# Each product ahead of a row maximum is multiplied twice in the first batch of an attention block

## What is computed

```python
xn = layernorm(x)                              # over channels
q, k, v = split(xn @ Wqkv.T + bqkv)            # 16 heads of 16
q, k = rope(q), rope(k)
att = softmax(where(causal, q @ k.T / 4, -inf))
s = (att @ v) @ Wo.T + bo
g = silu(sum_r(xn @ factors[r]) / sqrt(8) + bias)
out = x + s * g
```

## Time and profile before

| | before |
|---|---|
| three runs, us | 259.08, 259.93, 257.48 |
| median, us | 259.08 |
| the profiled execution, its time, us | 259.9 |
| its span, us | 258.1 |
| busy: PE, DVE, ACT, POOL, us | 233.8, 187.8, 140.2, 105.2 |
| mean granted clock of TensorE | 0.94 |

### The profile page before, as it was taken

The page is one execution under the profiler, slowest core; times in us unless marked ns, Lnnn a source line. Parts: engine busy times, 40 slices in busy tenths (PEclk is TensorE's granted clock), DMA queues, the critical chain, the costliest instruction groups (busy, mean ns, idle before and its releaser), DMA issues.

```text
span 258.1 us, 4983 instructions
## 1 busy us (share of the span) xinstructions
PE 233.8 (91%) x1717; PEld 141.2 (55%) x1717; DVE 187.8 (73%) x622; ACT 140.2 (54%) x268; POOL 105.2 (41%) x85
## 2 busy tenths in 40 slices
PE   5599969899966799999999999999998999999982
PEld 2388845465633335646675557464854474474552
DVE  7579789914799959479997868799968696941124
ACT  2511814667530157468547596667266467748840
POOL 8107868950386030030087200943565016019900
PEclk9799999869995569999999999999999799999999
DMA  6996301551024033000003520151016200002002
GB/s 195 353 325 180 69 0 60 201 200 35 0 98 149 6 122 124 5 3 0 3 5 106 198 70 5 65 187 39 3 35 205 93 6 0 4 5 84 3 0 81
DMA packets 15788, 21.42 MB, mean 83 GB/s; under 512 B 2068, under 2 KB 9236, under 8 KB 15764
## 3 DMA queue, kind: packets, MB, share of 16 engines
q1 hardware_dynamic: 14704, 19.54, 23.0%
q10 hardware_dynamic: 868, 1.05, 1.4%
q0 software_dynamic: 192, 0.52, 0.9%
HBM read 6.16 MB, written 2.10 MB: 32 GB/s over the span
## 4 chain that ended last, share of the span: by engine, by line
PE 67%; DVE 22%; DMA 3%; issue 3%; ACT 3%; ACTq 0%; DVEq 0%
PE o_ps L460 14%; DVE ring_ps L756 13%; PE ring_ps L564 11%; PE ring_ps L519 8%; PE ring_ps L575 7%; PE ring_ps L534 7%; PE ring_ps L500 7%; PE ring_ps L470 3%; PE ring_ps L510 3%; DMA probs<-wqk 2%; DVE rowmax L760 2%; PE ring_ps L550 2%; DVE rowmax L756 2%; PE ring_ps L608 2%; PE ring_ps L493 2%
## 5 line engine op out<-in xcount | busy, mean ns | idle before, releaser
L756 DVE CUSTOM_DVE_ANT_0 ring_ps<-ring_ps,later_k 128x512 f32<-128x512 f32 (+3 forms) x224 | 106.8, 543 | 17.7 <-PE ring_ps L534 17.4
L870 ACT ACTIVATE probs<-ring_ps 128x512 f32<-128x512 f32 x160 | 84.5, 603 | 28.2 <-PE ring_ps L575 23.5
L534 PE MATMUL ring_ps<-stack_k,stack_q 62*128 62x512 f32 (+3 forms) x256 | 44.0, 400 | 5.8 <-DVE rowmax L756 3.9
L564 PE MATMUL ring_ps<-stack_q,stack_k 64*128 64x128 f32 (+3 forms) x256 | 40.5, 371 | 3.5 <-DVE rowmax L756 1.5
L460 PE MATMUL o_ps<-probs,vaug 128*17 128x256 f32 (+3 forms) x496 | 37.9, 447 | 0.0
L534 PEld LDWEIGHTS ring_ps<-stack_k,stack_q 62*128 62x128 f32 x256 | 22.8, 197 | 24.2 <-issue 8.3
L756 DVE DVE_READ_ACCUMULATOR2_ANT rowmax<- 128x1 f32 x224 | 31.7, 141 | 0.0
L641 POOL TENSOR_TENSOR parts<-parts,by_sin 128x512 f32<-128x512 f32 x7 | 9.1, 1303 | 54.4 <-DVE by_sin L737 54.4
L564 PEld LDWEIGHTS ring_ps<-stack_q,stack_k 64*128 64x128 f32 x256 | 22.4, 194 | 16.2 <-issue 8.2
L575 PE MATMUL ring_ps<-ident_bf,later_k 128*128 128x256 bf16 (+1 forms) x160 | 29.1, 265 | 0.0
L519 PE MATMUL ring_ps<-wvg_sb,xnT 128*128 128x512 f32 x96 | 26.3, 419 | 0.8 <-DVE by_sin L737 0.7
(11 more groups left out here) (89 smaller groups left out, 279.9 us busy)
## 6 DMA issues: line engine op xcount, KB each, us to landing
stack_q<-parts SPq DMA_DIRECT2D x48, 128.0 KB, 2.6
stack_k<-parts SPq DMA_DIRECT2D x42, 128.0 KB, 2.6
probs<-factors SPq DMA_DIRECT2D x2, 1024.0 KB, 10.0
out<-result SPq DMA_DIRECT2D x8, 256.0 KB, 2.3
xbuf<-x SPq DMA_DIRECT2D x3, 512.0 KB, 8.2
xbuf<-x SPq DMA_DIRECT2D x2, 256.0 KB, 2.9
probs<-wqk ACTq DMA_DIRECT2D x2, 256.0 KB, 6.4
stack_k<-parts POOLq DMA_DIRECT2D x4, 128.0 KB, 3.8
```

The source lines that it names most:

```text
L534: mm = pe.matmul(ps[:, s * width:(s + 1) * width], qk[b % 2][0][rows, h // SIDES, tile * P:(tile + 1) * P], qk[b % 2][1][rows, h // SIDES, ...
L564: pe.matmul(ps[:, col:col + T - j * P], qk[b % 2][1][side(h), h // SIDES, j * P:(j + 1) * P], qk[b % 2][0][side(h), h // SIDES, j * P:T], ...
L756: last = dve.tensor_tensor_reduce(scores, scores, later_k[:, T - width:], 1.0, LOWEST, ALU.add, ALU.max, rowmax[:, tile, unit, column + s: ...
L870: act.activation(probs[:, chunk % PROB_SLOTS, :], ps[:, :], ACT.Exp, scale=float(HD) ** -0.5).then_inc(taken[kind], 1)
```

## The change

A table `REPEAT` gives, for each batch, how often the products of a maxima step are multiplied. In batch 0 it is 2, in the others 1. The extra products have the same operands and go to the same place in the same bank, just ahead of the old ones. As the old ones begin with `start=True`, they overwrite what the extra ones left, which nobody reads. No semaphore is added or moved.

```diff
--- before.py
+++ after.py
@@ -58,6 +58,7 @@
 
 WARM_UP = 12
 KEEP_WARM = 5
+REPEAT = (2, 1, 1, 1)
 VECTOR_MASKS_FROM = 1
 MAX_CHUNKS = 12
 EXP_CHUNKS = 10
@@ -526,6 +527,13 @@
                     wait_bank(pe, (kind, b, i + 1))
                     both = [(ring_bank((kind, b, n)), *max_chunk(n // MAX_CHUNKS, n % MAX_CHUNKS)) for n in (i, i + 1)]
                     count_heads = len(both[0][2])
+                    for s in [s for _ in range(REPEAT[b] - 1) for s in range(count_heads)]:
+                        for ps, tile, heads in both:
+                            h, width = heads[s], (tile + 1) * P
+                            rows = slice(side(h).start, side(h).start + DOT_ROWS)
+                            pe.matmul(ps[:, s * width:(s + 1) * width],
+                                      qk[b % 2][0][rows, h // SIDES, tile * P:(tile + 1) * P],
+                                      qk[b % 2][1][rows, h // SIDES, 0:width], start=(s == 0), stop=(s == count_heads - 1))
                     for s in range(count_heads):
                         for ps, tile, heads in both:
                             h, width = heads[s], (tile + 1) * P
```

## The result

The changed kernel takes 262.71 us, the median of four runs (261.75 to 263.43), beside 258.88 for the kernel before, also four runs (257.48 to 259.93). The ratio is 1.0164, with a 95% interval of 1.0118 to 1.0209: slower by 3.8 us, where the forecast was 258.3 us, 0.8 less than the 259.08 known then, and outside the range. A second series on another chip gave 1.0141 (1.0070 to 1.0212). The profiled execution took 262.7 us, with a span of 260.9.

The account below looks back on a forecast made before the run. After the first batch the kernel was taken to wait mostly for TensorE. Terms: 0.8 - 2.6 + 0.8 (swallowed) + 0.4 - 0.2 = -0.8 us, from 259.08 to 258.3 us; range 255.5 to 261.5, the forecast's own 257.2 to 259.8.

Parts of the forecast that it names:

- What bounds the kernel: After the first batch mostly waits for TensorE; early microseconds lost or won reach the end unless another engine swallows them.
- The price of a repeat: TensorE, batch 0: a repeated pair costs 0.23 us at width 512, 0.18 at 384 and 256, 0.17 at 128.
- The third rival: First block: a repeat's weights wait for the product ahead, 0.52 us a pair; +4.1, 263.2 us; chance 0.12.
- The first block: Heads 0 to 7, 32 to 49.4 us: the repeats make TensorE 0.8 us late, between nothing and 2.0.
- The second block: Heads 8 to 15, 67 to 81.5 us: two repeated pairs ahead of VectorE cost 0.4 us; other repeats hidden.
- The first dip: 50 to 57 us: repeats fill TensorE's gaps, the clock does not fall at 50, saving 2.6 us.
- What swallows it: VectorE waits for SyncE's transfers until 61.40, so at most 1.1 us of TensorE's lead survive; 1.0 taken, 0.8 swallowed.
- The second dip: Clock may hold until 81.5 us, then falls; L550 at 83.8 may win 0.4, half likely: -0.2 us.

Follow-up runs that it names:

- e1: Changed kernel with all 64 repeats, but VectorE's step `centre` of batch 2 moved later, behind the shift of unit 0: 258.69 us, ratio 0.9999 to the kernel before.
- e4: Kernel before with repeats only for heads 8 to 15 of batch 0, 32 of the 64: 259.34 us, ratio 1.0024.
- a2: The changed kernel itself measured once more, on another chip: 263.16 us beside 259.21 for the kernel before, ratio 1.0141.
- e10: Kernel before with repeats only for heads 0 to 7 of batch 0, `centre` in its old place: 262.36 us beside 259.21, ratio 1.0112.
- e7: Changed kernel with `centre` of batch 2 computed by four one-column operations with one tensor input each: 259.50 us beside 258.42 for the kernel before, ratio 1.0050.
- e2: Kernel before, no repeats, with `centre` of batch 2 moved later, behind the shift of unit 0: 258.08 us, ratio 0.9964.
- e3: Kernel before, no repeats, with `centre` of batch 2 put earlier, ahead of the four 384 reductions of group 1: 260.26 us, ratio 1.0058.

## Why the prediction was wrong

*What bounds the kernel, and that time lost or won early is carried to the end:* right for the loss. From 67 us on the profiled executions differ by a nearly constant 2.4 to 2.8 us. Wrong for a gain, as e1 shows below.

*The price of a repeat:* right for the wide pairs, 0.59 us for the three of the burst at 36.29. The narrow ones cost less than forecast: two 256 pairs put off the masks behind them by 0.24 us (0.67 from 39.46 to 40.13, where it was 0.43), two 128 pairs by 0.22, for 0.36 and 0.34. The third rival, whose 263.2 us is near the result, has the wrong mechanism: its 0.52 a pair did not occur, and TensorE was 0.74 late at the first scores, not 5.8.

*The first block, 0.8 us:* right in size, 0.74 in the changed kernel and 0.78 in e1. In part that is luck: the narrow pairs were priced too high, and the sum holds one of the second group's two 512 pairs only. *The second block, 0.4 us:* 0.34 in the profile (VectorE's first reduction at 77.05 before and 79.81 now is 2.76 apart, TensorE's scores ahead of the block 2.42), and 0.6 by the ratio of e4.

*The step that failed* is the sentence that the change adds work on TensorE "and nothing elsewhere: no wait, no transfer, no bank", and with it the sum of the first block, which ended at TensorE's own lateness. I followed VectorE's delay to the transpose and to the scores, but not to what stands on VectorE in between. The delay carried the step `centre` over a seam on GpSimd and made it 2.05 us longer (2.25 against 0.20). The rows were there: 48.97 with 0.20, and GpSimd's 46.80 and 49.15, which show a step that ended 0.02 us after a seam.

*The first dip, -2.6 us:* did not come. The stall left TensorE 1.84 us idle, and the clock fell right after, as it did behind the stall in a2 and e10. Where the same repeats run without the stall, in the profiles of e1 and e7, there is no dip, and L520 takes the 1.65 us that were forecast at 1.67. That the stall brings the dip is likely by this, not shown. And e2 has no dip either, without repeats, so the repeats are not shown to be what holds the clock.

*What swallows it:* the cap was meant for a lead and never came into play. VectorE's L743 (the old L735) did not stay at 61.40, and it waited for TensorE now and no longer for the transfers:

```profile
61.65 0.75 DVE L743 SCALAR_TENSOR_TENSOR parts<-ring_ps,bqk_sb,cos_t 128x512 f32<-128x512 f32 x1 [5.91 <-PE ring_ps L501]
```

Where there was a lead, in e1, it was 1.7 us and not 1.0, as VectorE began L743 at 60.68. Why the transfers were done sooner there is open.

*The second dip, -0.2 us:* L558 there took 1.01 as before; nothing was won. And e1 shows what I had not priced: the clock rose no sooner than before, so work that came earlier only ran longer at the low level. The lead of 1.7 us at 63.75 was 0.4 at 95.92 (0.16 by the rows, and the offset of 0.21).

So even with the stall out of the way (e1, 0.9999) the change brings nothing measurable.

Together: forecast -0.8; the stall adds 2.05; the dip that stayed adds 2.6; the part of it that would have been swallowed, 0.8, falls away; the 0.2 of the second dip is missing. -0.8 + 2.05 + 2.6 - 0.8 + 0.2 = 3.25 us, for 3.4 in the profiled spans without their offset and 3.8 in the medians.

Shown by runs are the stall, what lifts it (e1, e7), that it costs time without repeats (e3), and that it goes with the first block (e4, e10). e3 lost 1.5 us, with 0.8 to 2.2 by its interval, so the 2.05 us of its stall may have been carried whole. The sum above is a bookkeeping of one profiled execution of each kernel. In a2 that dip was half as long, and the loss was as large. How often an execution of the kernel before has the first dip is not on record, so the share of the 3.8 us that belongs to the clock rather than to the stall itself stays open.

## What to carry to other kernels

When a change delays an engine by a few tenths of a microsecond, go down its list for operations that share something with another engine, and see how near their starts are to a seam there; a step of four numbers a row can stand at the edge of two microseconds. Keep small operations with two SBUF inputs away from the critical order on VectorE while GpSimd works, or give them one input. And a lead won ahead of a low-clock stretch was worth next to nothing here (e1), as that stretch did not end earlier as well.

## What the runs showed of the hardware

A VectorE operation with two tensor inputs in SBUF waited for the end of GpSimd's running TENSOR_TENSOR, small as it was: a 128x4 operation took 2.25 us in the change (twice), 2.26 in e3 and e10 and 1.45 in e1, and in e1 and e3 it ended 0.02 to 0.03 us after GpSimd's operation. Four 128x1 operations with one tensor input, started at the same distance into the same operation, took 0.57 us together (e7), and the shift L776, with one input in SBUF, took 0.68 us beside the very operation that held the step in e1. Beside a MEMSET of GpSimd, which reads nothing, the step was not held; it took 0.15 us on batch 1 in the kernel before:

```profile
25.70 0.15 DVE L706 SCALAR_TENSOR_TENSOR centre<-moments,rstd 128x4 f32<-128x4 f32 x1
```

```profile
25.16 0.94 POOL L408 MEMSET stack_k<- 128x1024 f32 x1
```

The Trainium skill ("SBUF — State Buffer", "Who interferes with whom") says this: an instruction of VectorE with two SBUF inputs contends with one of GpSimd that reads SBUF, not with one that only writes it, and one with at most one SBUF input, outside the modes that use two ports, does not contend. The traces agree on all three, by the numbers above.

Weight loads did not wait for the product ahead of them on the same rows of the array: repeated pairs of width 384 follow one another after 0.18 us, which is the length of one load alone (0.183) and leaves no room for a product behind it.

TensorE's clock fell to the 1.2 GHz level in the kernel before and held in e2 after the same 3.15 busy microseconds of the 4.00 from 46 to 50 us, so the busy time of that stretch, as the profile shows it, did not tell which it would be.
